# Last attention of a twelve-stage kernel: gating on GpSimd behind each pair of steps, and the sum of the read parts in PSUM

## The chip, the cores and the metric

The kernel runs on one core of a Trainium2 chip, in one launch. The metric is the device time of one execution in microseconds (us). TensorE multiplies matrices, VectorE (DVE) and GpSimd (POOL) compute elementwise, ScalarE (ACT) evaluates functions and takes results out of PSUM, and SyncE (SP) issues transfers.

## The reference

A "macaron" stack of twelve sublayers on tokens of width 128 (2 sequences of 1024). The change touches the eleventh alone, the gated delta attention of the last layer (`_deltanet_forward`, MIX = 0.05). With x already normalised:

```python
q, k, v = silu(heads(Wq)), silu(heads(Wk)), silu(heads(Wv))
beta = sigmoid(x @ Wb.T); fd = sigmoid(x @ Wfd.T + bfd); sd = sigmoid(x @ Wsd.T + bsd)
def step(carry, inp):
    Sf, Ss = carry
    Sf = Sf * ft[..., None]; Ss = Ss * st[..., None]
    o = 0.5 * qt * (Sf + Ss)
    upd = bt[..., None] * kt * vt
    Sf = Sf + upd; Ss = Ss + upd
    Sf_new = Sf + MIX * Ss
    Ss = Ss + MIX * Sf
    return (Sf_new, Ss), o
g = sigmoid(x @ Wg.T)
return o * g @ Wo.T        # added to the residual x
```

## The kernel before, in words

The stage is `l3_attn`. Features lie on the 128 partitions, tokens along the free dimension. The 2048 tokens are 4 chunks of 512 (`CHUNKS`) for products, and 64 segments (`S`) of 32 steps (`L`) for the recurrence: all segments run the same step at once, each as if it started from zero, and a scan over the segments joins them afterwards.

- **Products.** TensorE multiplies each chunk by seven weights, ScalarE applies the function and writes the result. The last eight are the output gate `g` and the query `q`.
- **Step loop** (`dve_step`, 32 times, VectorE). `states` holds for the fast and the slow state (a = 0, 1) three rows (`K` = 3): row 0 is the state from a zero start, rows 1 and 2 are its factors of the two states at the segment's start. A step multiplies by the decay into `faded` (L3449), mixes fast and slow (L3452) and adds the key to row 0 (L3455), each waiting for the one before.
- **Read parts.** Behind each pair of steps (`PAIRS` = 16) TensorE adds fast and slow of `faded` with the identity (`pe_sum`, L3464), and ScalarE copies the sum to `read[:, :, :, 2p:2p+2]` (`act_sum`, L3469). `read` is [128, 3 parts, 64 segments, 32 steps], so two neighbouring elements in each 32 are written.
- **Scan** (`dve_scan`, VectorE). Five rounds with distances 1 to 16 over the 32 segments of a sequence: four products (L3480), two sums of one row (L3485), two sums of three rows (L3489). Then `starts` is copied (L3493).
- **Tail** (`dve_gate`, `dve_output`, `pe_out`, `dve_add`), chunk by chunk: the query times 0.5 and the gate (L3498), part 1 and part 2 times the starts (L3507, L3508), both added to part 0 (L3510, L3513), the sum times the gated query into `zt` (L3516). TensorE multiplies `zt` by `wo` (L3522), four matmuls a chunk, and VectorE adds the result to the residual `x` (L3528).

Each engine has a queue in the order of the code; semaphores (`wait_ge`, `then_inc`) order the engines. A barrier stands between stages: the last feed-forward stage begins when every engine has finished this one. GpSimd has only two short instructions here (`pool_root`).

Of the kernel before, what the change touches and what calls it, by code (L numbers as in the profile page):

```python
# [19 lines left out]
P = 128  # L20
# [3340 lines left out]
def l3_attn(core, area):  # L3361
# [4 lines left out]
    L, S, K = RA_STEP, RA_SEG, 3  # L3366
    PAIRS, SLOTS = L // 2, 4
    SEGS = CHUNK // L
    (made, taken, keyed, fed, gated, set_up, faded_done, mixed, stepped, sums, sums_taken, scanned, started, read_a, read_b, added_a, added_b,
     outputs, out_made, added) = (  # L3370
        core.sem(n) for n in (
            "product", "activated", "keys_taken", "gated", "biased_queries", "tables", "faded", "states", "steps", "sums_turned", "sums_taken",
            "vector_chain", "starts_set", "read", "read_second", "read_added", "read_whole", "outputs", "out_product", "added"))
    norm = ChunkNorm(core, x, y, 1e-5, begun=NEXT_CHUNKS)
    with ExitStack() as ctx:
        sb = lambda name, shape, dt=F32: ctx.enter_context(nc.sbuf_tensor(core.fresh(name), shape, dt))
# [5 lines left out]
        read = sb("ra_read", [P, K, S, L])  # L3382
        starts = sb("ra_starts", [P, 2, S])
        composed = sb("ra_composed", [P, 2, 2, K, S])
        seg = S // BATCH
        state2 = lambda t: t.rearrange("p a k s -> p a (k s)")
        by_seq = lambda t: t.rearrange("p k (b c) -> p k b c", b=BATCH)

        def chunk(c):
            return slice(c * CHUNK, (c + 1) * CHUNK)  # L3390

        def segments(c):
            return slice(c * SEGS, (c + 1) * SEGS)
# [78 lines left out]
        def dve_scan(dve):  # L3472
            link = Steps(dve, scanned)
            dve.wait_ge(*stepped.at(L))
            distance = 1
            while distance < seg:
                late, soon = slice(distance, seg), slice(0, seg - distance)
                for a in range(2):
                    for e in range(2):
                        last = nc.vector.tensor_tensor(by_seq(composed[:, a, e])[:, :, :, late],  # L3480
                                                       by_seq(states[:, a, 1 + e:2 + e, :])[:, :, :, late].to_broadcast([P, K, BATCH, seg - distance]),
                                                       by_seq(states[:, e])[:, :, :, soon], ALU.mult)
                link(last)
                for a in range(2):
                    last = nc.vector.tensor_tensor(by_seq(composed[:, a, 0, 0:1, :])[:, :, :, late], by_seq(composed[:, a, 0, 0:1, :])[:, :, :, late],  # L3485
                                                   by_seq(states[:, a, 0:1, :])[:, :, :, late], ALU.add)
                link(last)
                for a in range(2):
                    last = nc.vector.tensor_tensor(by_seq(states[:, a])[:, :, :, late], by_seq(composed[:, a, 0])[:, :, :, late],  # L3489
                                                   by_seq(composed[:, a, 1])[:, :, :, late], ALU.add)  # L3490
                link(last)
                distance *= 2
            nc.vector.tensor_copy(by_seq(starts[:])[:, :, :, 1:seg], by_seq(states[:, :, 0, :])[:, :, :, 0:seg - 1]).then_inc(started.handle, 1)  # L3493
            link.close()

        def dve_gate(dve, c):
            dve.wait_ge(*taken.at(made_by["wq", c]))
            nc.vector.scalar_tensor_tensor(out=q[:, chunk(c)], in0=q[:, chunk(c)], scalar=0.5, in1=g[:, chunk(c)], op0=ALU.mult,  # L3498
                                           op1=ALU.mult).then_inc(gated.handle, 1)

        def dve_output(dve, c):
            if c == 0:
                dve.wait_ge(*started.at(1))
                dve.wait_ge(*sums_taken.at(PAIRS))
            part = [read[:, n, segments(c), :] for n in range(K)]
            start = [starts[:, a, segments(c)].unsqueeze(2).to_broadcast([P, SEGS, L]) for a in range(2)]
            nc.vector.tensor_tensor(part[1], part[1], start[0], ALU.mult).then_inc(read_a.handle, 1)  # L3507
            nc.vector.tensor_tensor(part[2], part[2], start[1], ALU.mult).then_inc(read_b.handle, 1)  # L3508
            dve.wait_ge(*read_a.at(c + 1))
            nc.vector.tensor_tensor(part[0], part[0], part[1], ALU.add).then_inc(added_a.handle, 1)  # L3510
            dve.wait_ge(*read_b.at(c + 1))
            dve.wait_ge(*added_a.at(c + 1))
            nc.vector.tensor_tensor(part[0], part[0], part[2], ALU.add).then_inc(added_b.handle, 1)  # L3513
            dve.wait_ge(*added_b.at(c + 1))
            dve.wait_ge(*gated.at(c + 1))
            nc.vector.tensor_tensor(zt[:, chunk(c)], part[0].rearrange("p s l -> p (s l)"), q[:, chunk(c)], ALU.mult).then_inc(outputs.handle, 1)  # L3516

        def pe_out(pe, c):
            pe.wait_ge(*outputs.at(c + 1))
            for j in range(PER_CHUNK):  # L3520
                at = c * CHUNK + j * P
                last = nc.tensor.matmul(psum[:, c, j * P:(j + 1) * P], zt[:, at:at + P], w("wo"), start=True, stop=True)  # L3522
            last.then_inc(out_made.handle, 1)

        def dve_add(dve, c):
            tiles = slice(c * PER_CHUNK, (c + 1) * PER_CHUNK)
            dve.wait_ge(*out_made.at(c + 1))
            nc.vector.tensor_tensor(x[:, tiles, :], psum[:, c, :].rearrange("p (j n) -> p j n", j=PER_CHUNK), x[:, tiles, :],  # L3528
                                    ALU.add).then_inc(added.handle, 1)

        with nc.Block() as block:
            @block.gpsimd
            def _(pool):
                for c in range(CHUNKS):
                    norm.pool_root(pool, c)

            @block.tensor
            def _(pe):
                for c in range(CHUNKS):
                    norm.pe_turn(pe, c, turn_bank(c))  # L3540
                    if c:
                        pe_product(pe, "wk", c - 1)
                        pe_product(pe, "wv", c - 1)
                pe_product(pe, "wk", CHUNKS - 1)
                pe_product(pe, "wv", CHUNKS - 1)
                for name, c in runs[len(early):]:
                    pe_product(pe, name, c)
                for p in range(PAIRS):
                    pe_sum(pe, p)
                for c in range(CHUNKS):  # L3550
                    pe_out(pe, c)

            @block.scalar
            def _(act):
                nc.scalar.add_instruction(mybir.InstLoadActFuncSet(
                    name=nc.get_next_instruction_name(), act_func_set_id=SILU, engine=mybir.EngineType.Activation, ins=[], outs=[]))
                for c in range(CHUNKS):
                    norm.act_take(act, c, turn_bank(c))
                    if c:
                        act_product(act, "wk", c - 1, ACT.Silu)  # L3560
                        act_product(act, "wv", c - 1, ACT.Silu)
                act_product(act, "wk", CHUNKS - 1, ACT.Silu)
                act_product(act, "wv", CHUNKS - 1, ACT.Silu)
                for c in range(CHUNKS):
                    act_product(act, "wb", c, ACT.Sigmoid)
                for c in range(CHUNKS):
                    act_product(act, "wfd", c, ACT.Sigmoid, w("bfd"))
                for c in range(CHUNKS):
                    act_product(act, "wsd", c, ACT.Sigmoid, w("bsd"))
                for c in range(CHUNKS):  # L3570
                    act_product(act, "wg", c, ACT.Sigmoid)
                for c in range(CHUNKS):
                    act_product(act, "wq", c, ACT.Silu)
                for p in range(PAIRS):
                    act_sum(act, p)

            @block.vector
            def _(dve):
# [13 lines left out]
                for t in range(L):  # L3592
                    dve_step(dve, t)
                dve_scan(dve)
                dve_gate(dve, 0)
                dve_output(dve, 0)
                for c in range(1, CHUNKS):
                    dve_gate(dve, c)
                    dve_output(dve, c)
                    dve_add(dve, c - 1)  # L3600
                dve_add(dve, CHUNKS - 1)
        norm.close()
        set_up.done += 4
        made.done += len(runs)
        taken.done += len(runs)
        for tally in (faded_done, mixed, stepped):
            tally.done += L
        for tally in (sums, sums_taken):
            tally.done += PAIRS
        started.done += 1  # L3610
        for tally in (keyed, fed, gated, read_a, read_b, added_a, added_b, outputs, out_made, added):
            tally.done += CHUNKS


# [231 lines left out]
```

## Time and profile before

| | us |
|---|---|
| median of 3 runs (2495.49 to 2511.19) | 2499.46 |
| the profiled execution | 2497.42 |
| its span, first to last instruction | 2495.6 |
| the last attention, 2222.9 to 2329.4 | 106.5 |
| of it: step loop / scan / tail | 50.3 / 10.2 / 19.8 |
| busy in the whole span: PE, DVE, ACT, POOL | 2178.1, 1532.4, 1187.6, 376.9 |

Times in the trace count from the span's start. A matmul of f32 data shows as two records. PEld is the load of weights. In a group, "x16 | 13.2, 822" is the count, the busy us and the mean ns of one. In windows, the length is followed by the busy times of PE, PEld, DVE, ACT and POOL, then by the clock that TensorE was granted (1.00 is 2.4 GHz, 0.50 is 1.2 GHz), the DMA's share and GB/s.

### The profile page before, as it was taken

How to read it: one execution, taken by the hardware profiler on the slowest of the kernel's cores; microseconds unless marked ns; L12 is line 12 of the kernel's file. 1: busy time of each engine (PE TensorE's matmuls, PEld its weight loads, DVE VectorE, ACT ScalarE, POOL GpSimd, SP SyncE). 2: the span in 40 equal slices, each digit the busy share in tenths (PEclk: the TensorE clock that was granted, in tenths of full speed). 3: DMA queues.
4: the chain of work that ended last, by engine and by line, in shares of the span. 5: the costliest groups of instructions: out<-in, count | busy, mean ns of one | idle time of the engine just before them, and what ended most of it. 6: DMA issues, size and time to landing. Idle time of an engine off the chain costs nothing. (4 is left out here: it accounts for less than half of the span.)

```text
span 2495.6 us, 39864 instructions
## 1 busy us (share of the span) xinstructions
PE 2178.1 (87%) x15567; PEld 1186.5 (48%) x15567; DVE 1532.4 (61%) x2855; ACT 1187.6 (48%) x2084; POOL 376.9 (15%) x580
## 2 busy tenths in 40 slices
PE   6988987987988988998999999799668669995799
PEld 3665664664665664453222232244446554442345
DVE  7986986558987985016778787330586783038600
ACT  4764772355765762212577767532335533143221
POOL 4322331114322320002000000000113100000000
PEclk9999998998999999998799999999879889999799
DMA  3000000000000000002010100000001100000000
GB/s 137 4 6 3 4 6 8 1 35 16 5 7 1 4 6 28 0 0 71 21 30 21 30 21 21 10 0 1 5 1 38 52 1 8 0 1 0 0 0 17
DMA packets 39452, 38.80 MB, mean 16 GB/s; under 512 B 26882, under 2 KB 31618, under 8 KB 38498
## 3 DMA queue, kind: packets, MB, share of 16 engines
q1 hardware_dynamic: 38354, 34.90, 4.6%
q8 instruction: 125, 2.05, 0.3%
q0 software_dynamic: 912, 1.35, 0.2%
q14 instruction: 61, 0.50, 0.1%
HBM read 27.88 MB, written 4.46 MB: 13 GB/s over the span
## 5 line engine op out<-in xcount | busy, mean ns | idle before, releaser
L2250 DVE TENSOR_REDUCE fa_top<-psum 128x1 f32<-128x1024 f32 x256 | 305.1, 1221 | 76.9 <-PE psum L2193 75.9
L2239 ACT ACTIVATE fa_prob<-psum 128x512 f32<-128x512 f32 x512 | 278.8, 596 | 144.4 <-PE psum L2206 143.4
L549 DVE TENSOR_TENSOR scaled<-psum,area_b 128x512 f32<-128x512 f32 x16 | 11.1, 692 | 443.3 <-PE psum L518 443.3
L508 PE MATMUL psum<-hidden_b,area_b 128*128 128x512 f32 x512 | 221.7, 592 | 0.0
L508 PE MATMUL psum<-hidden_a,area_b 128*128 128x512 f32 x512 | 220.4, 592 | 0.0
L2193 PE MATMUL psum<-fa_stack_k,fa_stack_q 72*128 72x512 bf16 x512 | 204.4, 409 | 6.9 <-DMA fa_stack_k<-fa_ones 3.1
L2206 PE MATMUL psum<-fa_stack_q,fa_stack_k 74*128 74x512 bf16 x512 | 199.5, 393 | 10.0 <-ACT fa_prob L2239 4.4
L773 POOL TENSOR_TENSOR turn_a<-turn_a,turn_b 128x1024 f32<-128x1024 f32 x64 | 151.1, 2362 | 286.1 <-DVE turn_b L991 286.1
L790 PE MATMUL psum<-area_a,zt 128*128 128x512 f32 x256 | 136.1, 656 | 24.3 <-ACT k_t L922 14.3
L2206 PEld LDWEIGHTS psum<-fa_stack_q,fa_stack_k 74*128 74x128 bf16 x512 | 49.0, 97 | 225.7 <-ACT fa_prob L2239 196.3
L508 PEld LDWEIGHTS psum<-hidden_a,area_b 128*128 128x128 f32 x512 | 97.3, 190 | 122.5 <-issue 122.5
L508 PEld LDWEIGHTS psum<-hidden_b,area_b 128*128 128x128 f32 x512 | 96.6, 190 | 118.1 <-issue 118.1
L535 ACT ACTIVATE hidden_a<-psum,area_b 128x512 f32<-128x512 f32 x64 | 44.0, 687 | 204.1 <-PE psum L508 204.1
L2221 PE MATMUL psum<-fa_prob,fa_pair_v 128*32 128x512 f32 x1024 | 138.1, 612 | 0.0
L535 ACT ACTIVATE hidden_b<-psum,area_b 128x512 f32<-128x512 f32 x64 | 44.0, 688 | 169.5 <-PE psum L508 169.5
L320 POOL TENSOR_TENSOR rstd<-spread,minus_half 128x4 f32<-128x4 f32 x32 | 34.7, 1085 | 558.6 <-DVE spread L312 558.3
L1004 DVE TENSOR_TENSOR qk<-turn_a,norm 128x1024 f32<-128x1024 f32 x64 | 78.5, 1226 | 36.2 <-POOL norm L765 36.1
L790 PEld LDWEIGHTS psum<-area_a,zt 128*128 128x128 f32 x256 | 47.5, 204 | 107.3 <-ACT k_t L922 51.6
L987 DVE TENSOR_TENSOR turn_a<-psum,direct 128x1024 f32<-128x1024 f32 x64 | 78.4, 1225 | 30.1 <-ACT squares L896 29.9
L815 PE MATMUL psum<-ident,qk 128*128 128x128 f32 x512 | 72.0, 287 | 27.3 <-DVE turn_b L991 22.5
L1124 PE MATMUL psum<-glu_in,area_a 128*128 128x512 f32 (+1 forms) x192 | 88.8, 598 | 4.5 <-ACT glu_in L1111 4.5
L920 ACT COPY q_t<-psum 128x512 f32<-128x512 f32 x64 | 37.5, 586 | 109.7 <-PE psum L815 109.7
(365 smaller groups left out, 4288.4 us busy)
## 6 DMA issues: line engine op xcount, KB each, us to landing
area_b<-in_L_ffn SPq DMA_DIRECT2D x2, 2888.0 KB, 9.6
fa_stack_q<-fa_parts_dram SPq DMA_DIRECT2D x144, 32.0 KB
fa_stack_k<-fa_parts_dram SPq DMA_DIRECT2D x144, 32.0 KB
fa_parts_dram<-fa_prob SPq DMA_DIRECT2D x12, 256.0 KB, 2.6
area_a<-in_L_ffn SPq DMA_DIRECT2D x1, 2482.0 KB, 17.9
moved_halves<-y SPq DMA_DIRECT2D x16, 127.0 KB
area_b<-in_L_attn SPq DMA_DIRECT2D x1, 1880.5 KB, 19.5
area_a<-in_L_attn SPq DMA_DIRECT2D x1, 1538.0 KB, 6.5
```

The source lines that it names most:

```text
L508: last = nc.tensor.matmul(psum[:, 4 + n % 2, :], w(name)[:, k * TF_HID + m * P:k * TF_HID + (m + 1) * P], source[:, c, k, :], start=(k == ...
L535: nc.scalar.activation(out[:, c, m, :], psum[:, 4 + n % 2, :], ACT.Gelu, scale=w(scale)[:, m:m + 1]).then_inc(acted.handle, 1)
L773: nc.gpsimd.tensor_tensor(turn_a[:], turn_a[:], turn_b[:], ALU.add).then_inc(rotary_sums.handle, 1)
L790: last = nc.tensor.matmul(qk_banks[:, s, :], zt[:, 64 + n * P:64 + (n + 1) * P], wq[:, s * LA_INNER:(s + 1) * LA_INNER], start=True, stop= ...
L987: nc.vector.tensor_tensor(turn_a[:].rearrange("p (s h) d -> p s h d", s=2), qk_banks.rearrange("p s (h d) -> p s h d", d=D), direct[:, :, ...
L1004: nc.vector.tensor_tensor(qk[:], turn_a[:], norm[:, g % 2].unsqueeze(2).to_broadcast([P, 2 * H, D]), ALU.mult).then_inc(rotated.handle, 1)
L1124: last = nc.tensor.matmul(pair(u)[0:rows, part, :], w(f"w1{l}")[:, part * GLU_HID + at:part * GLU_HID + at + rows], ht[:, c * CHUNK:(c + 1 ...
L2193: last = nc.tensor.matmul(psum[:, 2 * j + half, :], stack_q[0:MAX_ROWS, head, t * P:(t + 1) * P], stack_k[0:MAX_ROWS, head, half * CHUNK:( ...
L2206: nc.tensor.matmul(psum[:, 4 + n % 2, :], stack_k[0:STACK, head, t * P:(t + 1) * P], stack_q[0:STACK, head, half * CHUNK:(half + 1) * CHUN ...
L2221: last = nc.tensor.matmul(psum[at:at + GROUP, 6 + g % 2, :], pair_v[:, g % 2, t, j, :], prob[:, (2 * s + j) % RING, half * CHUNK:(half + 1 ...
L2239: nc.scalar.activation(prob[:, (2 * s + j) % RING, half * CHUNK:(half + 1) * CHUNK], psum[:, 4 + n % 2, :], ACT.Exp, scale=float(D) ** -0. ...
L2250: nc.vector.tensor_reduce(top[:, g % 2, j, t:t + 1], psum[:, 2 * j:2 * j + 2, :].rearrange("p a n -> p (a n)"), AX.X, ALU.max, negate=True ...
```

## The change

The query gate leaves VectorE: GpSimd computes `q * g` for four chunks, without the factor 0.5, which goes into a halved copy of `wo` made by ScalarE at the stage's start. Behind each pair of steps GpSimd multiplies all three read parts of the pair by the gated query. After the scan VectorE multiplies part 1 and GpSimd part 2 by the starts, for the four chunks each. The two additions and the last gate are gone: TensorE multiplies the three parts one after the other by the halved `wo` and adds them in the same PSUM bank, 48 matmuls instead of 16; those of part 0 wait only for the last gated pair. In the last round of the scan only row 0 is kept.

```diff
+        half_wo = sb("ra_half_wo", [P, P])
...
             while distance < seg:
+                kept = K if 2 * distance < seg else 1
                 for a in range(2):
                     for e in range(2):
-                        last = nc.vector.tensor_tensor(by_seq(composed[:, a, e])[:, :, :, late],
...
+                        last = nc.vector.tensor_tensor(by_seq(composed[:, a, e, 0:kept])[:, :, :, late],
...
-        def dve_gate(dve, c):
-            dve.wait_ge(*taken.at(made_by["wq", c]))
-            nc.vector.scalar_tensor_tensor(out=q[:, chunk(c)], in0=q[:, chunk(c)], scalar=0.5, in1=g[:, chunk(c)], op0=ALU.mult,
-                                           op1=ALU.mult).then_inc(gated.handle, 1)
...
+        def pool_gate(pool, c):
+            pool.wait_ge(*taken.at(made_by["wq", c]))
+            nc.gpsimd.tensor_tensor(q[:, chunk(c)], q[:, chunk(c)], g[:, chunk(c)], ALU.mult).then_inc(gated.handle, 1)
+
+        def pool_gate_parts(pool, p):
+            pool.wait_ge(*sums_taken.at(p + 1))
+            part = read[:, :, :, 2 * p:2 * p + 2]
+            nc.gpsimd.tensor_tensor(part, part, q[:].rearrange("p (s l) -> p s l", l=L)[:, :, 2 * p:2 * p + 2].unsqueeze(1).to_broadcast([P, K, S, 2]),
+                                    ALU.mult).then_inc(parts_gated.handle, 1)
+
+        def start_part(vector, c, a):
+            part = read[:, 1 + a, segments(c), :]
+            return vector.tensor_tensor(part, part, starts[:, a, segments(c)].unsqueeze(2).to_broadcast([P, SEGS, L]), ALU.mult)
+
+        def pe_out(pe, c, n):
+            if n == 1:
+                pe.wait_ge(*started_a.at(c + 1))
+            if n == 2:
+                pe.wait_ge(*started_b.at(c + 1))
+            tokens = read[:, n].rearrange("p s l -> p (s l)")
             for j in range(PER_CHUNK):
                 at = c * CHUNK + j * P
-                last = nc.tensor.matmul(psum[:, c, j * P:(j + 1) * P], zt[:, at:at + P], w("wo"), start=True, stop=True)
-            last.then_inc(out_made.handle, 1)
+                last = nc.tensor.matmul(psum[:, c, j * P:(j + 1) * P], tokens[:, at:at + P], half_wo[:], start=(n == 0 and j == 0), stop=(n == K - 1),
+                                        skip_group_check=True)
+            if n == K - 1:
+                last.then_inc(out_made.handle, 1)
...
+                for c in range(CHUNKS):
+                    pool_gate(pool, c)
+                pool.wait_ge(*gated.at(CHUNKS))
+                for p in range(PAIRS):
+                    pool_gate_parts(pool, p)
+                pool.wait_ge(*parts_gated.at(PAIRS))
+                pool.wait_ge(*started.at(1))
+                for c in range(CHUNKS):
+                    start_part(nc.gpsimd, c, 1).then_inc(started_b.handle, 1)
...
+                pe.wait_ge(*halved.at(1))
+                pe.wait_ge(*parts_gated.at(PAIRS))
                 for c in range(CHUNKS):
-                    pe_out(pe, c)
+                    pe_out(pe, c, 0)
+                for c in range(CHUNKS):
+                    for n in range(1, K):
+                        pe_out(pe, c, n)
...
+                nc.scalar.mul(half_wo[:], w("wo"), 0.5).then_inc(halved.handle, 1)
...
+                dve.wait_ge(*parts_gated.at(PAIRS))
+                dve.wait_ge(*started.at(1))
+                for c in range(CHUNKS):
+                    start_part(nc.vector, c, 0).then_inc(started_a.handle, 1)
+                for c in range(CHUNKS):
+                    dve_add(dve, c)
```

GpSimd, around this stage, before: the stage lies between the first two branches.

```order
L3532 UNCONDITIONAL_BRANCH
L320 TENSOR_TENSOR rstd<-spread,minus_half 128x4 x2
L3531 UNCONDITIONAL_BRANCH
L566 UNCONDITIONAL_BRANCH
L320 TENSOR_TENSOR rstd<-spread,minus_half 128x4 x4
L555 UNCONDITIONAL_BRANCH
```

The same place after, with the semaphores waited for ("activated" is ScalarE's result, "sums_taken" a copied pair, "starts_set" the starts):

```order
L3532 UNCONDITIONAL_BRANCH [waits barrier_Pool_Activation_PE_DVE_SP_gather]
L320 TENSOR_TENSOR rstd<-spread,minus_half 128x4 [waits spread_ready] x2
L3500 TENSOR_TENSOR ra_q<-ra_q,ra_g 128x512 [waits activated] x4
L3505 TENSOR_TENSOR ra_read<-ra_read,ra_q 128x192x2 [waits sums_taken,biased_queries]
L3505 TENSOR_TENSOR ra_read<-ra_read,ra_q 128x192x2 [waits sums_taken] x15
L3510 TENSOR_TENSOR ra_read<-ra_read,ra_starts 128x512 [waits starts_set,outputs]
L3510 TENSOR_TENSOR ra_read<-ra_read,ra_starts 128x512 x3
```

24 instructions have come in: four query gates, 16 gates of pairs (384 elements each), four start products.

VectorE, the end of the stage before: the last chunk, and the last additions to x.

```order
L3498 SCALAR_TENSOR_TENSOR ra_q<-ra_q,ra_g 128x512
L3507 TENSOR_TENSOR ra_read<-ra_read,ra_starts 128x512
L3508 TENSOR_TENSOR ra_read<-ra_read,ra_starts 128x512
L3510 TENSOR_TENSOR ra_read<-ra_read 128x512
L3513 TENSOR_TENSOR ra_read<-ra_read 128x512
L3516 TENSOR_TENSOR zt<-ra_read,ra_q 128x512
L3528 TENSOR_TENSOR x<-psum,x 128x512 x2
```

After, from the last round of the scan to the end of the stage:

```order
L3482 TENSOR_TENSOR ra_composed<-ra_states 128x2x16 x4
L3487 TENSOR_TENSOR ra_composed<-ra_composed,ra_states 128x2x16 x2
L3491 TENSOR_TENSOR ra_states<-ra_composed 128x2x16 x2
L3495 COPY ra_starts<-ra_states 128x4x31
L3510 TENSOR_TENSOR ra_read<-ra_read,ra_starts 128x512 x4
L3528 TENSOR_TENSOR x<-psum,x 128x512 x4
```

Behind the copy of the starts VectorE has 8 instructions where it had 28, and the additions to x stand behind all start products.

TensorE, from the last products of the stage to its end:

```order
-L3413 MATMUL psum<-zt,area_a 128x512 x24
-L3464 MATMUL psum<-ra_faded,ident 128x384 x32
-L3522 MATMUL psum<-area_a,zt 128x128 x16
+L3414 MATMUL psum<-zt,area_a 128x512 x24
+L3465 MATMUL psum<-ra_faded,ident 128x384 x32
+L3520 MATMUL psum<-ra_half_wo,ra_read 128x128 x48
```

Three times as many output products, in the same place of the queue.

## Rows read from the trace of the kernel before

**Rows 1.** The page of the kernel before: its first line.

```profile
span 2495.6 us, 39864 instructions
```

**Rows 2.** Windows, core 0: us, busy (x count) per engine, granted clock, DMA.

```profile
2249.10:2299.40 50.30, 28.30 (x74) 12.77 (x74) 45.04 (x96) 17.52 (x24) 0.00 (x0) 1.00 0.00 0
2299.40:2309.60 10.20, 0.67 (x3) 0.05 (x1) 9.68 (x42) 0.82 (x1) 0.00 (x0) 0.66 0.00 0
2309.60:2329.40 19.80, 8.30 (x32) 7.12 (x32) 17.67 (x29) 0.00 (x0) 0.00 (x0) 0.50 0.00 0
```

**Rows 3.** Timeline, one late step of the loop: start, us, instruction [idle <-releaser].

```profile
2296.91 0.56 DVE L3452 SCALAR_TENSOR_TENSOR ra_states<-ra_faded 128x384 f32<-128x384 f32 x1
...
2297.50 0.29 DVE L3455 TENSOR_TENSOR ra_states<-ra_states,ra_k 128x128 f32<-128x128 f32 x1
2297.90 0.56 DVE L3449 TENSOR_TENSOR ra_faded<-ra_states,ra_decay_gates 128x384 f32<-128x384 f32 x1
```

**Rows 4.** Timeline, from the last sum to the stage's end.

```profile
2298.51 1.56 PE L3464 MATMUL psum<-ra_faded,ident 128*128 128x384 f32 x4 [1.61 <-DVE ra_faded L3449]
...
2309.39 0.22 DVE L3493 COPY ra_starts<-ra_states 128x124 f32<-128x124 f32 x1
...
2326.59 2.08 PE L3522 MATMUL psum<-area_a,zt 128*128 128x128 f32 x8 [2.45 <-DVE zt L3516]
2328.70 0.69 DVE L3528 TENSOR_TENSOR x<-psum,x 128x512 f32<-128x512 f32 x1 [1.56 <-PE psum L3522]
```

**Rows 5.** Groups of GpSimd by shape: count | busy us, mean ns | idle.

```profile
L759 POOL TENSOR_TENSOR refine<-refine,square_sum 128x16 f32<-128x16 f32 x64 | 14.3, 223 | 5.0
...
L2333 POOL TENSOR_TENSOR x<-x,area_a 128x512 f32<-128x512 f32 x4 | 5.1, 1264 | 0.0
```

**Rows 6.** Groups of VectorE by shape, 2249 to 2330.

```profile
L3508 DVE TENSOR_TENSOR ra_read<-ra_read,ra_starts 128x512 f32<-128x512 f32 x4 | 2.7, 684 | 0.0
...
L3480 DVE TENSOR_TENSOR ra_composed<-ra_states 128x96 f32<-128x96 f32 x4 | 0.8, 253 | 0.0
...
L3485 DVE TENSOR_TENSOR ra_composed<-ra_composed,ra_states 128x32 f32<-128x32 f32 x2 | 0.3, 186 | 0.0
```

**Rows 7.** Lines L1884 (ns min/median/max) and L1929, and both in the timeline.

```profile
L1884 DVE TENSOR_TENSOR ga_v_factor<-ga_values,ga_factor x14: 415/418/1475, 469.9 to 544.0; 128x256 f32<-128x256 f32 x14
...
469.89 1.48 DVE L1884 TENSOR_TENSOR ga_v_factor<-ga_values,ga_factor 128x256 f32<-128x256 f32 x1 [5.80 <-ACT ga_factor L1867]
...
469.81 2.68 POOL L1929 TENSOR_TENSOR x<-x,area_b 128x512 f32<-128x512 f32 x2
...
471.05 1.45 POOL L1929 TENSOR_TENSOR x<-x,area_b 128x512 f32<-128x512 f32 x1
...
L1929 POOL TENSOR_TENSOR x<-x,area_b x4: 1265/1268/1448, 467.4 to 471.0; 128x512 f32<-128x512 f32 x4
```

**Rows 8.** GpSimd behind VectorE: timeline at 22.5, and line L320.

```profile
22.48 1.23 DVE L1004 TENSOR_TENSOR qk<-turn_a,norm 128x1024 f32<-128x1024 f32 x1 [0.72 <-POOL norm L765]
...
L320 POOL TENSOR_TENSOR rstd<-spread,minus_half x32: 998/1012/2094, 5.8 to 2338.1; 128x4 f32<-128x4 f32 x32
```

**Rows 9.** Clock: windows of the next stage; its products 128x128 at 2449.5.

```profile
2334.00:2340.00 6.00, 5.83 (x13) 3.31 (x14) 5.62 (x30) 1.33 (x3) 2.12 (x3) 0.50 0.00 0
2341.00:2360.00 19.00, 19.00 (x50) 7.97 (x48) 7.82 (x11) 7.83 (x12) 0.00 (x0) 1.00 0.00 0
...
2449.54 3.73 PE L518 MATMUL psum<-area_b,hidden_a 128*128 128x128 f32 x32
```

**Rows 10.** Groups of ScalarE by shape, 2240 to 2330.

```profile
L3469 ACT COPY ra_read<-psum 128x384 f32<-128x384 f32 x16 | 13.2, 822 | 33.5 <-PE psum L3464 33.5
...
L3419 ACT ACTIVATE ra_beta<-psum 128x512 f32<-128x512 f32 x3 | 2.8, 1075 | 0.0
...
L3419 ACT ACTIVATE ra_q<-psum 128x512 f32<-128x512 f32 x4 | 2.1, 597 | 0.0
```

**Rows 11.** Timeline, ScalarE at the start of the stage.

```profile
2225.65 1.03 ACT L3419 ACTIVATE ra_v<-psum 128x512 f32<-128x512 f32 x1 [0.40 <-PE psum L3413]
```

More of the change, by code:

```diff
@@ L3368, in l3_attn @@
     SEGS = CHUNK // L
-    (made, taken, keyed, fed, gated, set_up, faded_done, mixed, stepped, sums, sums_taken, scanned, started, read_a, read_b, added_a, added_b,
-     outputs, out_made, added) = (
+    (made, taken, keyed, fed, gated, set_up, faded_done, mixed, stepped, sums, sums_taken, scanned, started, started_a, started_b, halved, parts_gated,
+     out_made, added) = (
         core.sem(n) for n in (
             "product", "activated", "keys_taken", "gated", "biased_queries", "tables", "faded", "states", "steps", "sums_turned", "sums_taken",
-            "vector_chain", "starts_set", "read", "read_second", "read_added", "read_whole", "outputs", "out_product", "added"))
+            "vector_chain", "starts_set", "read", "read_second", "read_added", "outputs", "out_product", "added"))
     norm = ChunkNorm(core, x, y, 1e-5, begun=NEXT_CHUNKS)
@@ L3477, in dve_scan @@
                 late, soon = slice(distance, seg), slice(0, seg - distance)
+                kept = K if 2 * distance < seg else 1
                 for a in range(2):
                     for e in range(2):
-                        last = nc.vector.tensor_tensor(by_seq(composed[:, a, e])[:, :, :, late],
-                                                       by_seq(states[:, a, 1 + e:2 + e, :])[:, :, :, late].to_broadcast([P, K, BATCH, seg - distance]),
-                                                       by_seq(states[:, e])[:, :, :, soon], ALU.mult)
+                        last = nc.vector.tensor_tensor(by_seq(composed[:, a, e, 0:kept])[:, :, :, late],
+                                                       by_seq(states[:, a, 1 + e:2 + e, :])[:, :, :, late].to_broadcast([P, kept, BATCH, seg - distance]),
+                                                       by_seq(states[:, e, 0:kept])[:, :, :, soon], ALU.mult)
                 link(last)
@@ L3488, in dve_scan @@
                 for a in range(2):
-                    last = nc.vector.tensor_tensor(by_seq(states[:, a])[:, :, :, late], by_seq(composed[:, a, 0])[:, :, :, late],
-                                                   by_seq(composed[:, a, 1])[:, :, :, late], ALU.add)
+                    last = nc.vector.tensor_tensor(by_seq(states[:, a, 0:kept])[:, :, :, late], by_seq(composed[:, a, 0, 0:kept])[:, :, :, late],
+                                                   by_seq(composed[:, a, 1, 0:kept])[:, :, :, late], ALU.add)
                 link(last)
@@ L3494, in dve_scan @@
             link.close()
-        def dve_gate(dve, c):
-            dve.wait_ge(*taken.at(made_by["wq", c]))
-            nc.vector.scalar_tensor_tensor(out=q[:, chunk(c)], in0=q[:, chunk(c)], scalar=0.5, in1=g[:, chunk(c)], op0=ALU.mult,
-                                           op1=ALU.mult).then_inc(gated.handle, 1)
[L3501 to L3516, printed above, removed]
@@ L3518, in pe_out @@
-        def pe_out(pe, c):
-            pe.wait_ge(*outputs.at(c + 1))
+        def pool_gate(pool, c):
[6 more added lines that the diff above has]
+                                    ALU.mult).then_inc(parts_gated.handle, 1)
@@ L3594, in _ @@
                 dve_scan(dve)
[L3595 to L3601, printed above, removed]
+                dve.wait_ge(*parts_gated.at(PAIRS))
[4 more added lines that the diff above has]
+                    dve_add(dve, c)
         norm.close()
@@ L3607, in l3_attn @@
             tally.done += L
-        for tally in (sums, sums_taken):
+        for tally in (sums, sums_taken, parts_gated):
             tally.done += PAIRS
         started.done += 1
-        for tally in (keyed, fed, gated, read_a, read_b, added_a, added_b, outputs, out_made, added):
+        halved.done += 1
+        for tally in (keyed, fed, gated, started_a, started_b, out_made, added):
             tally.done += CHUNKS
```

## The prediction

> **What bounds the kernel now.** I read the page's first line, then the windows of the last attention, then the order of its instructions, and last the rows that price VectorE and GpSimd side by side.
>
> The span is 2495.6 us and the profiled execution took 2497.42 us, so 1.8 us lie around the span [rows 1]. The three times shown run from 2495.49 to 2511.19 with a median of 2499.46, which is 2.0 above this execution. My sum is made against 2497.42. About 1% (25 us) is what a measurement of this kernel can tell from no change.
>
> The change touches three stretches of one stage [rows 2]. In the step loop (2249.1 to 2299.4) VectorE is busy for 45.04 of 50.30 us, while TensorE has 28.30, ScalarE 17.52 and GpSimd 0.00. In the scan (to 2309.6) VectorE has 9.68 of 10.20, and in the tail (to 2329.4) 17.67 of 19.80. So VectorE sets the length of all three, and GpSimd is free. The loop has 32 steps of 1.58 us, each a chain of three dependent VectorE instructions of 0.56, 0.56 and 0.29 us with gaps of 0.03 to 0.1 us [rows 3]. Every one of them reads two tensors of SBUF: states and decay, the two halves of `faded`, states and keys. The same is true of all products and sums of the scan. That fact decides this case.
>
> In the tail each chunk costs VectorE six instructions of about 0.68 us (q gate, two start products, two additions, gate) and the addition to x. It begins at the copy of `starts`, at 2309.39, and the last addition starts at 2328.70 [rows 4]. TensorE's work for a chunk follows by 2.1 us and is covered except for the last one.
>
> **What the tail gives back.** Between the copy of `starts` and the end there are now 19.8 us. Afterwards VectorE has four start products (part 1), GpSimd four (part 2), TensorE adds the parts, and four additions to x follow, three of them under TensorE's work.
>
> GpSimd's product of 128x512 is priced by two rows of the same form: 1.27 us for 512 elements, 0.22 us for 16 [rows 5]. VectorE's is 0.68 [rows 6]. Whether the two run side by side is the question. In the opening part of another stage the VectorE product `ga_v_factor`, which reads two SBUF tensors and takes 415 to 418 ns, took 1475 ns when it was issued at 469.89, 0.08 us behind the start of a GpSimd product with two SBUF inputs; it ended 0.29 us after that product. The GpSimd product behind it took 1448 instead of 1265 ns, and ended 1.13 us after VectorE's [rows 7]. In the other order, a GpSimd instruction that takes 1012 ns took 2094 behind a VectorE product of 1.23 us [rows 8]. So they take turns: neither goes on while the other is in its data. For chunk after chunk that makes 0.71 for VectorE's first, then 1.13 for GpSimd and 0.55 for VectorE in turn: GpSimd's fourth product ends at 0.71 + 4 x 1.13 + 3 x 0.55 = 6.9 us behind the starts.
>
> TensorE then has the last part of the last chunk. In the tail four 128x128 products show as 8 records in 2.08 us, at a granted clock of 0.50, the 1.2 GHz level [rows 2, 4]; 32 such records at the full clock took 3.73 us in the last feed-forward stage, 0.11 each [rows 9]. At the full clock the end is 6.9 + 0.1 + 8 x 0.11 + 0.3 (the drain, 2.08 less 8 x 0.22) + 0.7 = 8.9 us. The gain is 19.8 - 8.9 = 10.9 us.
>
> I take the full clock for this reason. The first 16 products (part 0) wait only for the last gated pair. They begin during the scan and last 3.6 us at the full clock, 7.1 at half, so they end about when the starts are set and the other 32 products follow. In the next stage TensorE's steady work from 2334 had the low clock until 2340 and the full one from then on [rows 9]. Here it would have as much steady work before and at the starts.
>
> **The last scan round** works on one row of states instead of three. Four products go from 0.25 to 0.19 us and two sums likewise, by the 32-element row of the same scan [rows 6]: 6 x 0.065 = 0.4 us gained.
>
> **What the loop pays.** GpSimd gets four products 128x512 for the query gate (they wait for ScalarE's `ra_q`, in the third to sixth step) and 16 gates of 128x384, one behind each pair. By a line through 16 and 512 elements a gate takes 0.22 + 368 x 0.0021 = 1.00 us. A pair takes 3.16 us, so GpSimd keeps up, but each instruction stops the step chain once. By `ga_v_factor` the loss is 1475 - 418 = 1.06 for an instruction of 1.27, that is its length less 0.21 [rows 7]. When GpSimd waits for VectorE first, its part behind VectorE's end is its length less 0.13; VectorE's next ends its 384 elements (0.40 us, read off 0.29 for 256) and 0.02 later, where alone it would need 0.03 + 0.56. That is the length less 0.30. I take 0.25 between them: 16 x 0.75 = 12.0 us and 4 x 1.0 = 4.0 us, together 16.0, with 15.1 and 16.9 as ends. The 16th gate falls into the scan, whose instructions have two SBUF inputs too, so it costs the same.
>
> The Trainium skill (SBUF — State Buffer, "Who interferes with whom") says that the second to issue "fully blocks" until the first one ends, when VectorE has two SBUF inputs and GpSimd reads SBUF. By that rule to the letter each instruction costs its whole length, 16 x 1.00 + 4 x 1.27 = 21.1 us, and the time would be 2507. The rows bear out the blocking and give back a fifth of a microsecond each time.
>
> **What costs nothing.** The half of `wo` on ScalarE comes in front of its first activation; between its first two activations ScalarE waits 0.40 us for a product anyway [rows 11]. If that cover were gone it would be 0.3 us. TensorE's 32 additional products run under the scan and under GpSimd's products. Behind GpSimd's new waits nothing else is queued before the next stage. Taking the query gate and the two additions off VectorE is already inside the tail's difference.
>
> **Sum.** +16.0 - 10.9 - 0.4 = +4.7 us: 2497.4 + 4.7 = 2502.1 us.
>
> **Rivals.**
> (a) TensorE stays at half clock through the tail. Then its 64 records of parts 1 and 2 bound it: 64 x 0.22 = 14.2, the tail is 0.7 + 14.2 + 0.3 + 0.7 = 15.9, and the gain 3.9 instead of 10.9: 2509 us. For it: the clock fell when TensorE ran out of work at 2300 and stayed down through the whole tail (0.66, then 0.50) [rows 2]; and the slowed loop leaves TensorE idle for longer between two pairs. Against it: the steady work named above.
> (b) The gate of a pair is slower than a dense product of its size, since it touches two neighbouring elements in every 32. ScalarE, which writes the same tensor `ra_read` with such strides, takes 822 ns for 384 elements and 1075 for 512 into `ra_beta`, against 597 into the dense `ra_q`, 1.8 times as long [rows 10]. If GpSimd pays the same, a gate takes 1.8 us, each costs 0.8 more, and the time is 2502.1 + 12.7 = 2515 us. This is the case that ends clearly on the slow side; from 2.3 us a gate on it would be over 1%. Against it: every pair of elements lies side by side, and GpSimd's rate for two inputs is slow already. The Trainium skill (GPSIMD Engine Reference, "Performance pitfalls for Q7 kernels") gives 50% more per element for reads with steps over 8 bytes; by that a gate takes 1.5 us and the time is 2510. No row here shows it.
> (c) GpSimd's gates slip beside the step chain and neither waits. The loop then loses nothing, and the tail is bound by TensorE, 0.7 + 7.1 + 0.3 + 0.7 = 8.8: 2497.4 - 11.0 - 0.4 = 2486 us. Against it stand rows 7 and 8; for it only that a chain with gaps has not been seen beside GpSimd.
>
> **How the numbers follow.** Forecast 0.58; (a) 0.15; (b) 0.13; (c) 0.09; anything else, such as a slowed loop that moves a later stage, 0.05. The forecast spans 2499 to 2505 by the ends of the loss and the spread of the times. The range goes on to (a) and to (b) at 2515 on top, and stops short of (c) below: 2492 to 2516. What is left out is (c), (a) and (b) together, and part of the rest, some 0.17. No case but a gate of over 2.3 us reaches 1%: faster 0.01, same 0.95, slower 0.04.
>
> **What would show it.** In the changed kernel's trace: 16 of the 96 VectorE instructions of the loop and scan should last about 0.8 us longer than the others of their line, and about four by 1.0; the loop should be 15 us longer. GpSimd's gates should last 1.0 to 1.5 us, waiting included. The last attention should end 9 us behind the copy of `starts`, with TensorE's clock at 1.00 there. If no VectorE instruction is stretched, (c) holds and my main term falls. If the gates are 1.8 us, (b); if the clock is 0.50 behind the starts, (a). The forecast would be plainly wrong if the loop's loss were under 10 or over 25 us.

## The result: 0.3% slower, by the terms named, with one of them too small

The changed kernel's median is 2508.5 us (2504.05 to 2511.48 in seven runs); the kernel before gave 2499.46 (2495.49 to 2511.19 in seven). The ratio is 1.0031 with a 95% interval of 1.0017 to 1.0046, that is some 7.7 us more (4.2 to 11.5); the two medians by themselves lie 9.0 apart. That is within the 1% of the prediction, but the interval excludes that nothing changed. The profiled execution took 2506.78 us.

The windows of the same three stretches, cut at the changed kernel's own times (loop, scan, tail), with the columns of [rows 2]:

```profile
span 2505.0 us, 39992 instructions
...
2251.60:2318.90 67.30, 39.39 (x74) 16.66 (x74) 62.06 (x96) 17.46 (x24) 24.70 (x19) 0.77 0.00 0
2318.90:2329.70 10.80, 6.54 (x35) 5.23 (x33) 10.26 (x41) 0.83 (x1) 1.37 (x1) 0.69 0.01 2
2329.70:2338.70 9.00, 7.42 (x64) 7.23 (x64) 7.63 (x9) 0.00 (x0) 5.92 (x4) 1.00 0.00 0
```

Against [rows 2] the loop grew from 50.3 to 67.3 us, the scan from 10.2 to 10.8, and the tail shrank from 19.8 to 9.0. VectorE has the same 96 instructions in the loop and 17.0 us more of busy time: no new gaps, longer instructions. I took the same stretches to a hundredth of a microsecond from the starts and ends in each trace. "Prelude" goes from ScalarE's table load at the start of the stage to the first step, and "stage" from that table load to the next stage's:

| kernel | prelude | loop | scan | tail | stage | span |
|---|---|---|---|---|---|---|
| before | 26.18 | 50.27 | 10.24 | 19.77 | 107.12 | 2495.6 |
| after | 26.26 | 67.30 | 10.84 | 9.00 | 114.05 | 2505.0 |

So the stage pays 6.9 us. The other 2.4 us of the two spans' difference lie ahead of the stage, in code that is the same. In the runs of this study that code took between 2219.9 and 2227.5 us up to the table load, so for the single executions below the stage is compared and not the total.

The lines of the step loop and the first products of the scan (duration in ns, shortest/median/longest):

```profile
L3450 DVE TENSOR_TENSOR ra_faded<-ra_states,ra_decay_gates x32: 557/558/1544, 2251.6 to 2317.4; 128x384 f32<-128x384 f32 x32
...
L3453 DVE SCALAR_TENSOR_TENSOR ra_states<-ra_faded x32: 557/558/1564, 2252.2 to 2318.0; 128x384 f32<-128x384 f32 x32
...
L3456 DVE TENSOR_TENSOR ra_states<-ra_states,ra_k x32: 291/292/1270, 2252.8 to 2318.6; 128x128 f32<-128x128 f32 x32
...
L3482 DVE TENSOR_TENSOR ra_composed<-ra_states x20: 185/330/1323, 2318.9 to 2328.6; 128x186 f32<-128x186 f32 x4, 128x180 f32<-128x180 f32 x4, 128x168 f32<-128x168 f32 x4, 128x144 f32<-128x144 f32 x4
...
L3500 POOL TENSOR_TENSOR ra_q<-ra_q,ra_g x4: 1312/1555/1581, 2255.4 to 2259.7; 128x512 f32<-128x512 f32 x4
...
L3505 POOL TENSOR_TENSOR ra_read<-ra_read,ra_q x16: 1144/1192/1536, 2261.3 to 2321.2; 128x384 f32<-128x384 f32 x16
...
L3510 DVE TENSOR_TENSOR ra_read<-ra_read,ra_starts x4: 693/1530/1537, 2329.8 to 2333.4; 128x512 f32<-128x512 f32 x4
L3510 POOL TENSOR_TENSOR ra_read<-ra_read,ra_starts x4: 1490/1492/1556, 2329.9 to 2334.3; 128x512 f32<-128x512 f32 x4
```

The medians are those of before, the maxima 0.98 to 1.0 us above them. Exactly 20 VectorE instructions are stretched, as many as GpSimd has in that time: 6 fades, 7 mixes, 6 additions and 1 scan product, by 0.79 to 1.01 us each, 18.03 in all. One pair shows it plainly:

```profile
2295.68 0.29 DVE L3456 TENSOR_TENSOR ra_states<-ra_states,ra_k 128x128 f32<-128x128 f32 x1
2296.08 1.54 DVE L3450 TENSOR_TENSOR ra_faded<-ra_states,ra_decay_gates 128x384 f32<-128x384 f32 x1
2297.66 0.56 DVE L3453 SCALAR_TENSOR_TENSOR ra_states<-ra_faded 128x384 f32<-128x384 f32 x1
...
2296.06 1.14 POOL L3505 TENSOR_TENSOR ra_read<-ra_read,ra_q 128x384 f32<-128x384 f32 x1 [3.40 <-ACT ra_read L3470]
```

GpSimd's gate began 0.02 us ahead of a fade and ran its 1.14 us undisturbed; the fade ended 0.42 us behind it and lasted 1.54 instead of 0.56. Where GpSimd begins in the middle of a VectorE instruction its own record is the longer one, up to 1.54: it waits first.

In the tail four start products on GpSimd take 5.92 us and three of VectorE's four are stretched by 0.84. TensorE and ScalarE (start, us, instruction, idle before it):

```profile
2322.67 5.23 PE L3520 MATMUL psum<-ra_half_wo,ra_read 128*128 128x128 f32 x32 [2.46 <-POOL ra_read L3505]
2330.58 7.42 PE L3520 MATMUL psum<-ra_half_wo,ra_read 128*128 128x128 f32 x64 [2.69 <-DVE ra_read L3510]
...
2226.63 0.31 ACT L3571 ACTIVATE ra_half_wo<-area_a 128x128 f32<-128x128 f32 x1
2226.85 1.02 ACT L3420 ACTIVATE ra_k<-psum 128x512 f32<-128x512 f32 x1
2228.06 1.03 ACT L3420 ACTIVATE ra_v<-psum 128x512 f32<-128x512 f32 x1 [0.20 <-PE psum L3414]
```

The 64 records behind the starts take 7.42 us without a gap, 0.116 each, the full clock of [rows 9]. GpSimd's last product ends at 2335.80, TensorE's at 2338.00: the end of the stage hangs on TensorE. The half of `wo` took 0.31 us, ScalarE's wait shrank from 0.40 to 0.20, and the prelude grew by 0.08.

### The profile page after: what moved, and what is told of

Same layout as the page of the kernel before. It is cut to its first block and busy times, and to the rows that moved or that the text cites. A ratio compares the mean times of both kernels' runs of the same rounds, so it can differ in the third digit from the quotient of the medians.

```text
span 2505.0 us, 39992 instructions
## 1 busy us (share of the span) xinstructions
PE 2195.0 (88%) x15631; PEld 1196.9 (48%) x15631; DVE 1539.4 (61%) x2835; ACT 1186.9 (47%) x2085; POOL 408.1 (16%) x604
## 5 line engine op out<-in xcount | busy, mean ns | idle before, releaser
L320 POOL TENSOR_TENSOR rstd<-spread,minus_half 128x4 f32<-128x4 f32 x32 | 34.7, 1084 | 460.1 <-DVE spread L312 459.8
L850 PE MATMUL psum<-ident,prob 128*128 128x128 f32 x512 | 68.8, 278 | 24.5 <-ACT prob L931 24.4
```

## The experiments

Two things were to be settled: why each gate costs 0.89 us and not 0.75, and whether it is turn-taking for reads at all. The rivals were that the gate's writes, its strides or its tile `ra_read` (which ScalarE writes beside it) do the harm.

**One suspected cost by itself: reads, on own tiles.** To the kernel before, nothing is added but 16 dense GpSimd products behind the pairs, on tiles that nobody reads:

```diff
+                for p in range(PAIRS):
+                    pool.wait_ge(*sums_taken.at(p + 1))
+                    pool.wait_ge(*own.at(2 + p))
+                    nc.gpsimd.tensor_tensor(own_c[:], own_a[:], own_b[:], ALU.mult).then_inc(own.handle, 1)
```

> The kernel before, with 16 GpSimd products of 384 dense elements on tiles of its own added, each issued behind one copied pair; nobody reads their result. Theory T1 (VectorE and GpSimd take turns when VectorE reads two SBUF tensors and GpSimd reads SBUF): 16 VectorE instructions of loop and scan are stretched by 0.75 to 0.95 us, the loop is 62 to 65 us instead of 50.3, the whole about 13 us longer. Rival T2 (the stretching comes from the changed kernel's data flow: shared tensors, waits, strided access to the read parts): nothing is stretched and the loop stays at 50.3. If a dense product lasts as long as the changed kernel's gate alone (1.14 us), the stride costs GpSimd nothing.

The time was 2508.6 us against 2497.22 for the kernel before. GpSimd's line, and one product with the addition that it meets:

```profile
L3543 POOL TENSOR_TENSOR ra_own_c<-ra_own_a,ra_own_b x16: 991/1134/1368, 2256.2 to 2312.7; 128x384 f32<-128x384 f32 x16
...
2291.94 1.15 POOL L3543 TENSOR_TENSOR ra_own_c<-ra_own_a,ra_own_b 128x384 f32<-128x384 f32 x1 [1.10 <-ACT ra_read L3471]
...
2292.27 0.96 DVE L3457 TENSOR_TENSOR ra_states<-ra_states,ra_k 128x128 f32<-128x128 f32 x1
```

The addition issued in the middle of the product ended 0.14 us behind it and lasted 0.96 instead of 0.29. Sixteen instructions were stretched, 7 additions by 0.68, 2 mixes by 0.68, 6 fades by 0.74 to 0.79 and one scan product by 0.80: 11.6 us. The loop took 61.04 us, a microsecond under the range set for it, since each costs 0.73 and not 0.75 or more. So neither the tile nor the strides are the cause. The strides set the size: at its shortest the dense product takes 0.991 us where the gate takes 1.144.

**The same with writes alone.** GpSimd's product becomes a fill of 1216 elements:

```diff
+                    nc.gpsimd.memset(own_c[:], 1.0).then_inc(own.handle, 1)
```

> As the run before, but each GpSimd instruction is a fill of 1216 elements of a tile of its own, about 1.15 us long, which reads no SBUF. T1: no VectorE instruction is stretched, the loop stays at 50.3 us. Rival T3 (any GpSimd instruction of that length holds VectorE up, through SBUF as such or through its writes): 16 stretched instructions and a loop of 62 to 65 us.

It took 2500.11 us:

```profile
L3543 POOL MEMSET ra_own_c<- x16: 1111/1111/1113, 2258.6 to 2303.7; 128x1216 f32 x16
...
L3451 DVE TENSOR_TENSOR ra_faded<-ra_states,ra_decay_gates x32: 557/558/559, 2251.8 to 2300.6; 128x384 f32<-128x384 f32 x32
```

The fills last nearly as long as the gates (1.11 us) and the longest fade is 559 ns; the loop is 50.26 us. Writes don't harm, and the theory that blames them falls.

**The other side: VectorE's inputs.** The running states of the loop go to PSUM (bank 7, the sums keep banks 4 to 6), and only the last step writes `ra_states`. All else is the changed kernel:

```diff
+        running = psum[:, 7, 0:2 * K * S].rearrange("p (a k s) -> p a k s", a=2, k=K)
...
+            to = running if t + 1 < L else states
+            nc.vector.tensor_tensor(slot, running[:], decay[:, :, t, :].unsqueeze(2).to_broadcast([P, 2, K, S]),
...
-            if p >= 4:
-                pe.wait_ge(*sums_taken.at(p - 3))
+            if p >= 3:
+                pe.wait_ge(*sums_taken.at(p - 2))
```

> The changed kernel with the running states of the step loop in PSUM, so that two of the three VectorE instructions of a step (fade, add) read one SBUF tensor and the third (mix) still reads two. T1: only mixes are stretched in the loop, by up to 0.9 us each, fades and adds never; the loop is about 58 to 63 us instead of 67.3. T3 (any instruction beside GpSimd): fades, mixes and adds are stretched alike and the loop stays at 67.

This execution took 2491.49 us. Of the line of additions:

```profile
L3458 DVE TENSOR_TENSOR psum<-psum,ra_k x31: 298/299/300, 2250.8 to 2301.4; 128x128 f32<-128x128 f32 x31
L3458 DVE TENSOR_TENSOR ra_states<-ra_states,ra_k x1: 1157/1157/1157, 2302.9 to 2302.9; 128x128 f32<-128x128 f32 x1
```

The 31 additions that read the states in PSUM keep their length. The 32nd, behind the last mix, reads `ra_states` in SBUF, so it has two SBUF inputs again, and it is stretched by 0.86 us. The same kernel was then timed in ten executions:

> The kernel of the run states_psum again, timed. T1: its stage is 101.1 us against 107.1 before and 114.05 changed, so it should be 6 us faster than the kernel before (ratio 0.9976, 0.996 to 0.999) and some 13 us faster than the changed one. T3 (nothing to do with what VectorE reads; the single look was a lucky one): ratio 1.00 or above.

Its median was 2490.99 us (2487.66 to 2493.56, ten runs) beside 2498.44 of the kernel before (fourteen runs): a ratio of 0.9972, 0.9963 to 0.9981. It beats the kernel before, and by way of the two ratios the changed one too. Of this kernel the windows, the three lines of the loop, and one gate with the fade beside it:

```profile
2246.10:2299.90 53.80, 35.33 (x73) 15.19 (x73) 48.53 (x96) 17.61 (x24) 25.37 (x19) 0.84 0.00 0
2299.90:2310.70 10.80, 8.27 (x35) 6.93 (x33) 10.27 (x41) 0.83 (x1) 1.15 (x1) 0.54 0.00 0
2310.70:2319.70 9.00, 7.42 (x64) 7.23 (x64) 7.63 (x9) 0.00 (x0) 5.92 (x4) 1.00 0.00 0
...
L3452 DVE TENSOR_TENSOR ra_faded<-psum,ra_decay_gates x32: 557/558/558, 2246.1 to 2298.4; 128x384 f32<-128x384 f32 x32
...
L3455 DVE SCALAR_TENSOR_TENSOR psum<-ra_faded x31: 566/566/1578, 2246.7 to 2297.4; 128x384 f32<-128x384 f32 x31
...
L3458 DVE TENSOR_TENSOR psum<-psum,ra_k x31: 299/299/300, 2247.3 to 2298.0; 128x128 f32<-128x128 f32 x31
...
2288.88 1.36 POOL L3507 TENSOR_TENSOR ra_read<-ra_read,ra_q 128x384 f32<-128x384 f32 x1 [3.44 <-ACT ra_read L3472]
...
2289.64 0.56 DVE L3452 TENSOR_TENSOR ra_faded<-psum,ra_decay_gates 128x384 f32<-128x384 f32 x1
```

Fades and additions now read one tensor from PSUM, and not one of the 63 is stretched, though GpSimd works beside them as before: the gate at 2288.88 is in its data when the fade at 2289.64 runs in 0.56 us. Only the mix still reads two SBUF tensors (the halves of `faded`), and only mixes stretch, seven of them by 0.08 to 1.01 us, with the rest 3.0 us together; the scan product loses 0.97, as in the changed kernel. The loop costs 3.5 us more than before instead of 17.0, these 3.0 and 0.5 for the place of the states (next run). I had expected more mixes to be hit (58 to 63 us, and it was 54.46 in the single execution). What counts is how many of an instruction's inputs lie in SBUF. The Trainium skill (SBUF — State Buffer, "Who interferes with whom") states it so: with at most one SBUF input and outside its 2-port modes, VectorE doesn't contend with GpSimd, and a GpSimd instruction that only writes doesn't contend with a VectorE instruction of two SBUF inputs. Both halves agree with these runs on VectorE's side, at 558 and 559 ns.

**Is it PSUM that is quicker?** The same move, in the kernel before, with no work on GpSimd:

> The kernel before with only the states in PSUM, without any GpSimd work in the loop. T1: the place of the states alone changes next to nothing, the loop is 50 to 51 us and the stage 107.1 within 0.7, so the gain of the run before comes from keeping GpSimd out of VectorE's way. Rival T5 (VectorE's chain is simply faster on PSUM): a loop of 46 us or less.

It took 2500.37 us, the loop 50.75: 0.5 us longer than before, since mixes take 566 ns instead of 557 and additions 299 instead of 291. The move by itself gains nothing, and that rival falls.

**When the gate comes.** GpSimd also waits for the end of a mix, so that each gate begins at the same point of a step, 0.11 us into the addition behind that mix:

```diff
+            pool.wait_ge(*mixed.at(4 + c))
...
+            pool.wait_ge(*mixed.at(min(max(2 * p + 4, 8 + p), L)))
```

> The changed kernel with one more wait in front of each GpSimd product of the loop: it starts only when a mix of the step chain has ended. States stay in SBUF, so each following VectorE instruction reads two SBUF tensors. T1: the moment does not matter, each GpSimd product still stops one instruction (now always the add behind the mix), 19 or 20 are stretched, the loop is 67 us within 1.5. Rival T4 (only a GpSimd instruction that comes in the middle of a VectorE one hurts, by waiting itself and then holding on): a loop clearly shorter, under 62 us.

It took 2504.52 us:

```profile
2249.30:2314.30 65.00, 36.00 (x74) 15.20 (x74) 59.72 (x96) 17.58 (x24) 22.85 (x19) 0.79 0.00 0
2314.30:2326.00 11.70, 4.52 (x35) 3.75 (x33) 11.15 (x42) 0.84 (x1) 2.24 (x2) 0.89 0.01 1
2326.00:2336.60 10.60, 8.95 (x64) 8.76 (x64) 7.75 (x9) 0.00 (x0) 5.92 (x4) 0.80 0.00 0
...
L3450 DVE TENSOR_TENSOR ra_faded<-ra_states,ra_decay_gates x32: 557/1340/1444, 2249.4 to 2312.8; 128x384 f32<-128x384 f32 x32
```

Again 20 are stretched: 17 fades, by 0.78 to 0.89, one mix and two products of the scan. I had named the addition, but it runs when the gate comes; GpSimd waits for its end, and the fade behind it pays. The loop loses 14.7 us in 18 instructions and is 64.97, half a microsecond under my 65.5 to 68.5. The place decides a tenth of a microsecond of each loss, not whether it is paid: a loop of under 62 us, as the rival had it, did not come. Since the gates still came in the middle of an addition, this run alone doesn't rule that rival out. The pair shown from the changed kernel does: at 2296.06 the addition had ended (2295.97), the gate came into the gap, waited for nothing, and the fade lost 0.99 all the same. So it is with five of the products on own tiles, which came into such a gap and cost the fade 0.79 each. And what the loop gave back, the scan (+0.9) and the tail (+1.5) took: the stage is 114.04 us again.

**Both together**, states in PSUM and the gates behind a mix's end (but for the last gate):

> States in PSUM, and each GpSimd product of the loop but the last starts only when a mix has ended, so that it runs beside the add and the fade, which read one SBUF tensor each. From one mix's end to the next's start there is 1.0 us, and GpSimd's product lasts 1.15 us or more with its wake-up. T1: each product (19 of them in the loop) reaches a little into the next mix, which is stretched by 0.1 to 0.3 us, none by more than 0.4; the loop is 53 to 56 us. Rival T6 (turn-taking lasts only as long as the data phase, 0.9 us): no mix is stretched and the loop is 51 us.

It took 2498.56 us. The loop was 54.28 us: 18 mixes lose 0.15 to 0.46 each (one more than the 0.4 set as the most), 3.5 us together, where the few of the kernel without that wait lost 3.0. So placing the gates gains nothing, and the rival by which no mix is stretched falls. GpSimd's own records, with additions and fades of one SBUF input beside them, are 1.27 us for the query gates, the length of [rows 5], and 1.17 to 1.20 for most gates of a pair, a little over their shortest 1.14; why these are longer stays open. But the scan took 11.61, since two gates fall to it and two of its instructions lose 0.9 and 0.7, and the tail 10.82. TensorE's products here and in the kernel of the ten executions:

```profile
2311.23 3.81 PE L3525 MATMUL psum<-ra_half_wo,ra_read 128*128 128x128 f32 x32 [2.50 <-POOL ra_read L3510]
2320.44 9.25 PE L3525 MATMUL psum<-ra_half_wo,ra_read 128*128 128x128 f32 x64 [5.41 <-DVE ra_read L3515]
```

```profile
2303.65 6.76 PE L3522 MATMUL psum<-ra_half_wo,ra_read 128*128 128x128 f32 x32 [2.23 <-POOL ra_read L3507]
2311.56 7.42 PE L3522 MATMUL psum<-ra_half_wo,ra_read 128*128 128x128 f32 x64 [1.15 <-DVE ra_read L3512]
```

With the clock still up, part 0 is done in 3.81 us; TensorE then idles for 5.41, the clock falls, and the 64 records on which the end hangs take 9.25. With part 0 at the low clock for all but its end it takes 6.76, the idle time is 1.15 and the 64 records take 7.42. In this pair of kernels the faster beginning goes with the slower end.

**No GpSimd in the loop.** VectorE gates each pair itself, straight from the sums in PSUM in place of ScalarE's copy, two instructions a pair, and gates the queries; GpSimd keeps the start products:

```diff
+            for l in range(2):
+                last = nc.vector.tensor_tensor(read[:, :, :, 2 * p + l], psum[:, 4 + p % 4, l * K * S:(l + 1) * K * S].rearrange("p (k s) -> p k s", k=K),
+                                               q[:].rearrange("p (s l) -> p s l", l=L)[:, :, 2 * p + l].unsqueeze(1).to_broadcast([P, K, S]), ALU.mult)
```

> The changed kernel with both gates on VectorE: the query gate behind step 4, and the gate of a pair straight out of PSUM in place of ScalarE's copy (two instructions of 192 elements, which write with a step of 32 elements). GpSimd has only its four start products. T1: nothing is stretched in loop and scan; a pair's gate costs 0.5 to 0.7 us on VectorE, the loop is 59 to 63 us, scan and two gates 11 to 12, the tail 9: a stage of 106 to 110 us, near the kernel before and 4 to 8 below the changed one. T3: the same loss as with GpSimd, a loop of 67 or more.

It took 2505.33 us:

```profile
2253.70:2314.50 60.80, 34.26 (x73) 14.72 (x73) 57.03 (x127) 5.17 (x9) 0.00 (x0) 0.83 0.00 0
2314.50:2326.60 12.10, 8.21 (x36) 6.59 (x34) 11.58 (x47) 0.00 (x0) 0.00 (x0) 0.60 0.01 2
2326.60:2337.20 10.60, 9.04 (x64) 8.85 (x64) 7.71 (x8) 0.00 (x0) 5.91 (x4) 0.84 0.00 0
...
2291.36 0.29 DVE L3456 TENSOR_TENSOR ra_states<-ra_states,ra_k 128x128 f32<-128x128 f32 x1
2291.57 0.91 DVE L3510 TENSOR_TENSOR ra_read<-psum,ra_q 128x192 f32<-128x192 f32 x2
2292.40 0.55 DVE L3450 TENSOR_TENSOR ra_faded<-ra_states,ra_decay_gates 128x384 f32<-128x384 f32 x1
...
L3510 DVE TENSOR_TENSOR ra_read<-psum,ra_q x32: 458/508/527, 2265.0 to 2318.7; 128x192 f32<-128x192 f32 x32
...
2319.26 6.17 PE L3526 MATMUL psum<-ra_half_wo,ra_read 128*128 128x128 f32 x32 [2.73 <-DVE ra_read L3510]
2327.45 9.04 PE L3526 MATMUL psum<-ra_half_wo,ra_read 128*128 128x128 f32 x64 [2.02 <-DVE ra_read L3516]
```

No instruction of the loop waits for GpSimd, which has none there. The two instructions of a pair fall into the gap in which the chain waits for its own addition and overlap each other, so the fade begins 1.04 us behind the addition instead of 0.40: a pair costs 0.64 us, though each instruction shows 0.51. Thirteen pairs (8.3) and the four query gates (2.2) make the 10.5 us of the loop. Three more add 2.3 to the scan (12.13 against the changed kernel's 10.84 less its stretch of 0.98); two of these stand between instructions with no gap to fall into, and cost 0.80 each. That is 12.8 us against the 18.0 that the same gates cost from GpSimd. The stage is only 3.7 us shorter, 110.38, a little over the 106 to 110 expected, since the tail took 10.62 and not 9: its 64 records took 9.04 us. The clock had risen at 2324 during part 0, and was still up while TensorE idled; it fell 0.2 us after the 64 records began (granted 0.82 from 2327 to 2328, then 0.50) and came back at 2331. Here TensorE had idled for only 2.02 us, less than the 2.69 of the changed kernel, where the clock stayed up.

The stretches of all kernels (us, as in the table above):

| kernel | prelude | loop | scan | tail | stage |
|---|---|---|---|---|---|
| own reads | 26.23 | 61.04 | 11.03 | 19.77 | 118.71 |
| own writes | 26.16 | 50.26 | 10.23 | 19.77 | 107.07 |
| states in PSUM, no gates | 26.33 | 50.75 | 10.26 | 19.78 | 107.77 |
| after, states in PSUM (ten executions) | 26.20 | 53.75 | 10.83 | 9.00 | 100.43 |
| after, gates behind a mix | 26.18 | 64.97 | 11.70 | 10.53 | 114.04 |
| both | 26.36 | 54.28 | 11.61 | 10.82 | 103.73 |
| gates on VectorE | 26.20 | 60.78 | 12.13 | 10.62 | 110.38 |

## Why the prediction was right, and by how much it was off

The forecast was 2502.1, that is +4.7 us; the stage shows +6.9 and the ratio +7.7 (4.2 to 11.5). The sign, the mechanism and the range (2492 to 2516) held, and so did "within 1%".

**What the loop pays** is the term that was mis-sized: 16.0 us, with 16.9 as its upper end, against 18.03 (17.0 in the loop, 1.0 in the scan). The four query gates were right: behind them four instructions in a row lose 0.94 or 0.95 each, 1.0 was said. The 16 gates lose 14.2 us, 0.89 each and not 0.75. The step that failed is the length of a gate: a line through dense shapes gave 1.00 us (a dense product of that size does take 0.99), and at its shortest it takes 1.14. The deduction from the length, taken as 0.25, was right on the average: 1.144 - 0.889 = 0.26 for the gates and 0.991 - 0.725 = 0.27 for the products on own tiles, with 0.14 to 0.35 as its extremes.

**What the tail gives back**: 10.9 said, 10.8 measured, partly by luck. I had GpSimd's fourth product as what ends last, at 6.9 us behind the starts. It ended at 6.1, because its part behind VectorE's end was 0.91 us each time and not 1.13, and TensorE's 7.42 us of steady products, which start 0.84 behind the starts, ended last. So the path to the end was wrong, and the sum hardly moved because the two chains were 8.9 and 8.8 us in my own numbers (the second in the rival without blocking).

**TensorE's clock** came out as said: it rose during the products of part 0, which show 5.23 us, between the 3.6 and 7.1 of the prediction, and was 1.00 in the tail. But I had the other products follow at once, and TensorE idled for 2.69 us before them; that the clock held through this pause was luck, since in another kernel it fell behind a shorter one. How near rival (a) was, the last three kernels of the table show: there the clock was down when the 64 records began or fell 0.2 us later, and the tail is 1.5 to 1.8 us longer. It is not the 7 us that I gave, since the clock came back while they ran. What makes it fall in one kernel and stay in another stays open: the idle time alone doesn't order them (2.02 us with a fall, 2.69 without).

**The last scan round** is 1.55 us before and 1.16 after: 0.4, as said. **The half of `wo`** cost 0.08 of a microsecond and not nothing.

**The rivals.** (b), strides: they cost something, 0.15 us a gate, not 0.8. By the Trainium skill (GPSIMD Engine Reference, "Performance pitfalls for Q7 kernels") I had allowed 1.5 us for a gate; the measured 1.14 says that pairs of neighbours don't pay that price. (c) falls: with two SBUF inputs on either side there was no gate for which VectorE did not wait. The rule of the full block (on that page of the Trainium skill, SBUF — State Buffer, it stands in the closing section, "Summary: rules for kernel authors") charges the whole length: with the shortest records as lengths 16 x 1.144 + 4 x 1.27 = 23.4 us, where 18.0 were lost.

## What to carry to other kernels

An idle GpSimd is not free beside a VectorE-bound chain: when both read two SBUF tensors, price each GpSimd instruction at its own length less about a quarter of a microsecond, on VectorE's account. Look first at whether one of VectorE's inputs can live in PSUM: here that turned 17.0 us of loss into 3.5 and a slower kernel into a faster one, without making a single instruction quicker. A small gate may even be cheaper on VectorE itself (0.64 us a pair here where its chain has a gap, 0.80 where it has none) than on the idle engine beside it (0.89).

## What the runs showed of the hardware that was not expected

- GpSimd's product of 384 elements takes 991 ns dense, and 1144 ns when it reads and writes pairs of neighbours at every 32nd place, each at its shortest: 15% more. ScalarE's writes with such strides took 1.8 times the dense time per element [rows 10].
- A GpSimd fill of 1111 ns beside VectorE instructions with two SBUF inputs costs them at most 2 ns.
- A mix that writes to PSUM takes 9 ns more than one that writes to SBUF, and an addition that reads and writes there 8 ns; a fade that reads one input from there costs nothing more (558 ns either way).
- Of two kernels with the same TensorE work behind the starts, the one whose part 0 ran at the full clock and then idled for 5.41 us needed 9.25 us for it (granted clock 0.78 in the tail), the one whose part 0 ran at the low clock for all but its end and ended 1.15 us ahead needed 7.42 (1.00).
